# Two outer products and a remainder trade places in the prologue of a fused signature, attention and mixture-of-experts kernel

## The reference

```python
dx = jnp.transpose(x[:, 1:] - x[:, :-1], (1, 0, 2))
def step(levels, v):
    e = [v]
    for k in range(1, d):                       # d = 4
        e.append(_outer(e[-1], v) / (k + 1))
    new = []
    for k in range(d):
        acc = levels[k] + e[k]
        for i in range(k):
            acc = acc + _outer(levels[i], e[k - 1 - i])
        new.append(acc)
    return tuple(new), jnp.concatenate(new, axis=-1)
_, sigs = jax.lax.scan(step, init, dx)
h = jnp.transpose(sigs, (1, 0, 2)) @ W.T + b
```

## Time and profile before

| | before |
|---|---|
| median of 3 runs | 641.4 us (641.23 to 641.78) |
| the profiled execution | 641.93 us |
| its span | 640.1 us |
| PE busy | 615.5 us (96%) |
| DVE busy | 428.1 us (67%) |
| POOL busy | 320.9 us (50%) |
| ACT busy | 289.6 us (45%) |

### The profile page before, as it was taken

How to read it: one execution, slowest core, us unless ns; L and a number is a source line. 1 busy time by engine, 2 the same in 40 slices (tenths; PEclk the granted TensorE clock), 3 DMA queues, 4 the chain that set the end, 5 groups by cost and what they waited for, 6 DMA issues and landing times.

```text
span 640.1 us, 13350 instructions
## 1 busy us (share of the span) xinstructions
PE 615.5 (96%) x4085; PEld 517.7 (81%) x4085; DVE 428.1 (67%) x1093; ACT 289.6 (45%) x640; POOL 320.9 (50%) x336
## 2 busy tenths in 40 slices
PE   6889999999999999999999999999989999999993
PEld 4667888887888887888888787888768999999992
DVE  6977767767777766777776678788556535666450
ACT  4334444544444445343444434444465445666341
POOL 2365544554544454554455455445864502666663
PEclk9999999999999999999999999999999999999998
DMA  8620433344543334343334434111233732434330
GB/s 303 240 106 21 107 82 82 86 117 93 114 116 82 82 97 114 85 108 90 82 82 109 105 90 108 38 37 39 70 93 98 233 105 64 54 58 52 43 47 2
DMA packets 69901, 59.80 MB, mean 93 GB/s; under 512 B 6512, under 2 KB 58608, under 8 KB 69488
## 3 DMA queue, kind: packets, MB, share of 16 engines
q1 hardware_dynamic: 63232, 55.21, 33.3%
q0 software_dynamic: 6640, 4.22, 4.8%
HBM read 16.79 MB, written 26.30 MB: 67 GB/s over the span
## 4 chain that ended last, share of the span: by engine, by line
PE 87%; DVE 6%; POOL 3%; issue 2%; ACT 1%; DMA 0%; SPq 0%; DVEq 0%; POOLq 0%
PE bank L1303 80%; PE bank L1515 2%; PE bank L1360 2%; POOL sorted_rows L510 1%; POOL z L495 1%; POOL z L497 1%; DVE z L923 1%; PE bank L1618 1%; DVE whigh L818 1%; PE bank L1409 1%; PE bank L1418 0%; DVE h L822 0%; PE bank L1364 0%; DMA h<-x_prev 0%; DVE u L868 0%
## 5 line engine op out<-in xcount | busy, mean ns | idle before, releaser
L1303 PE MATMUL bank<-whigh,uth 128*128 128x512 f32 x512 | 167.3, 407 | 1.5 <-issue 1.3
L1303 PEld LDWEIGHTS bank<-whigh,uth 128*128 128x128 f32 x512 | 91.7, 189 | 27.2 <-issue 8.1
L1303 PE MATMUL bank<-whigh,utl 128*128 128x512 f32 x256 | 101.2, 395 | 0.0
L584 POOL DMA_INDIRECT out<-xvo,ids x39 | 61.5, 1577 | 62.9 <-ACT xvo L773 55.8
L504 POOL TENSOR_TENSOR rstd<-rstd,powers 128x1 f32<-128x1 f32 x64 | 35.3, 551 | 113.7 <-DVE rstd L910 65.6
L495 POOL TENSOR_TENSOR z<-z 128x512 f32<-128x512 f32 x32 | 40.8, 1275 | 70.5 <-DVE z L923 70.5
L1303 PE MATMUL bank<-xT,qkw 128*128 128x128 f32 x512 | 63.3, 277 | 0.0
L659 ACT ACTIVATE prob<-prob 128x512 f32<-128x512 f32 x32 | 20.2, 633 | 93.3 <-DVE prob L1050 93.3
L1303 PEld LDWEIGHTS bank<-xT,qkw 128*128 128x128 f32 x512 | 59.6, 192 | 0.7 <-issue 0.4
L1303 PEld LDWEIGHTS bank<-whigh,utl 128*128 128x128 f32 x256 | 48.1, 188 | 11.3
L490 POOL TENSOR_TENSOR e3l<-e,e3h 128x512 fp32r<-128x512 f32 x31 | 40.0, 1292 | 26.8 <-DVE xn L944 26.4
(11 more groups left out here) (236 smaller groups left out, 1364.6 us busy)
## 6 DMA issues: line engine op xcount, KB each, us to landing
sorted_rows<-blank SPq DMA_DIRECT2D x24, 709.5 KB, 6.1
xvp<-xvo SPq DMA_DIRECT2D x128, 128.0 KB, 2.3
w<-w_t SPq DMA_DIRECT2D x1, 4096.0 KB, 12.1
w<-w_high SPq DMA_DIRECT2D x4, 512.0 KB, 6.3
x_columns<-x2t SPq DMA_DIRECT2D x32, 64.0 KB, 1.6
xg_in<-x_columns SPq DMA_DIRECT2D x8, 256.0 KB, 4.1
out<-h SPq DMA_DIRECT2D x8, 256.0 KB, 2.2
levels<-w_t SPq DMA_DIRECT2D x1, 2048.0 KB, 10.5
```

Of the source, the lines that this page charges most:

```text
L584: nc.gpsimd.indirect_dma_start(out=out[:, :], out_offset=bass.IndirectOffsetOnAxis(ap=ids[:, tile:tile + 1], axis=0), in_=y[:, 2 if j == S ...
L1303: return T.matmul(out_, lhsT, rhs, start=start, stop=stop)
```

## The change

Three places move. On DVE, the fourth outer product `level2(3)` goes from behind `level2(2)` to behind `features_lo(0)`. On POOL, in the prologue only and for tile 2 only, the call `level3_rest(2)` is written out with its two operations exchanged, and the remainder no longer waits for `xn_ready`. On DVE, `level4(2)` goes ahead of `add_s2(3)`. No operation is added or removed, and only the order and one wait differ.

```diff
@@ -552,7 +552,11 @@
             add_channels(0)
             level3(2)
             root(0, ln1, 0)
-            level3_rest(2)
+            pool.wait_ge(e3_hi, 3)
+            G.tensor_tensor(e3l[:], e3[:], e3h[:].bitcast(F32), ALU.subtract).then_inc(e3_lo, 1)
+            pool.wait_ge(u4_sb, 2)
+            G.tensor_tensor(by3(g4), spread(g3[:, 2:3, :], 3, [P, 1, C2, CHANNELS]),
+                            spread(vh[:, 2:3, :], 2, [P, 1, C2, CHANNELS]), ALU.mult).then_inc(g4_ready, 1)
             pool.wait_ge(norm_step, SQUARED_STEP)
@@ -892,7 +896,6 @@
             level2(1)
             level4(0)
             level2(2)
-            level2(3)
 
             def one(ap):
@@ -1090,6 +1093,7 @@
             features_lo(0)
+            level2(3)
             signature_lo(0)
@@ -1131,9 +1135,9 @@
             made = nstep(V.tensor_tensor(nrm[:, 3:4], wu_out[:], B[5][:, DIM + 1:DIM + 2], ALU.mult))
             assert made == SUMS_STEP
+            level4(2)
             made = add_s2(3)
             assert made == SMALL_STEPS
-            level4(2)
             x_lo(0)
```

## The result

The changed kernel takes 643.34 us (median of 13 runs, 642.51 to 644.12) against 641.41 us in the same session: ratio 1.0027, 95% interval 1.0018 to 1.0035, so 1.9 us slower (1.2 to 2.2). 643.0 had been forecast, in a range of 641.5 to 643.6. The profiled execution took 643.41 us, its span is 641.6 us.

What follows compares the result with a forecast made beforehand. The prediction took DVE's queue, with POOL between, to bound the prologue. Delays of 0.40 and 1.17 us, with 0 for the third edit, gave 1.57, so 641.4 + 1.6 = 643.0 us, range 641.5 to 643.6 (eight in ten).

Steps and rivals of the forecast that it cites:

- first edit, DVE's queue: Prologue, DVE: with `level2(3)` behind `features_lo(0)`, the next operation starts at 18.01 in place of 17.61, 0.40 us later.
- moved product, duration: DVE at about 17.0 us: outer product `level2(3)`, held by POOL's `e3l` until 17.53, takes about 1.0 us.
- `xn` longer: DVE from 37.17 us: `xn`, held by POOL's `e3l` in place of `g4`, ends at 38.03, 0.21 us later.
- first `nrm`: DVE behind `xn`: the first tiny product, held by POOL's `g4`, takes about 1.1 us rather than 0.15.
- second edit, DVE's queue: DVE at `add_s2(2)`: starts at 39.12 in place of 37.95, 1.17 us later, as is everything up to `weigh(1, 1)`.
- third edit: DVE: `level4(2)` ahead of `add_s2(3)` is the same work in another order and does not wait: 0.
- `accumulate(1)`: PE's piece at 46.80 us, released by POOL behind DVE's `weigh(1, 1)`: comes at 48.4, late by both DVE delays.
- DVE's queue is the bound: Prologue: DVE's queue with POOL between, not PE, bounds it; the rival that PE's waits are the bound, 639.9 us, had 0.06.
- disputed step: DVE behind `xn`: a tiny 128x1 product is held by POOL like a large one; rival, not held, 642.0 us, chance 0.22.
- PE's slack: PE's 0.5 us wait ahead of 46.80: PE's earlier work may shift by some tenths without moving the end.
- the sum: Whole kernel: DVE's delays of 0.40 and 1.17 us add up to 1.57 us, with nothing from `level4(2)`.
- the prediction's last sign of being wrong: PE at 46.80 us: the prediction is wrong if this start moves by anything other than 0.40 + 1.17 = 1.57 us.

Runs made afterwards that it cites:

- g4_waits: The changed kernel with one wait added, so POOL's `g4` of tile 2 may not start before `xn`: 643.07 us against 642.07 for the kernel before, ratio 1.0015.
- fill: The changed kernel with 14 added, unread products in PE's two waits of the prologue: 642.35 us against 641.20 for the kernel before, ratio 1.0014.
- nrm_early: The changed kernel with the three `nrm` products moved ahead on DVE, behind the copy of `wu_out`: 641.51 us against 641.20 for the kernel before, ratio 1.0002.
- b_only: The kernel before with only POOL's `e3l` put ahead of `g4`, without the wait on `xn_ready`: 642.73 us against 642.07, ratio 1.0013.
- e3l: Not a run but a code name: POOL's operation that makes the remainder by subtraction, put ahead of `g4` for tile 2 in the changed kernel.

## Why the prediction held, and where it fell short

| step (us) | forecast | in the trace of the changed kernel |
|---|---|---|
| first edit, DVE's queue | +0.40 | +0.39 |
| moved product, duration | 1.0 | 1.02 |
| `xn` longer | +0.21 | 0.87 for 0.65, +0.22 |
| first `nrm` | 1.1 | 1.04 |
| second edit, DVE's queue | +1.17 | +1.11 |
| third edit | 0 | 0 |
| PE's clock | not thought of | +0.55 |
| `accumulate(1)` | +1.57 | +2.06 |
| median of the runs | +1.6 | +1.9 |

**DVE's queue is the bound.** Shown: PE began its first projection 0.55 us early behind the anchor and waited 1.26 us at `vow` instead. The three edits alone moved DVE's `weigh(1, 1)` by 0.40, 1.05 and 0.70 and `accumulate(1)` by 0.40, 1.62 and 0.70; the 0.57 that are over in the second are the clock's. In all seven changed orders whose trace has the clock up, PE still waited 0.5 us for POOL at `accumulate(1)`.

**The tiny product is held like a large one.** This was the disputed step, with a chance of 0.22 against it. `g4_waits` settles it: the same product at the same place takes 0.15 us when `g4` starts 0.17 later. It is `g4`'s turn that costs, and not the place behind `xn`.

**The step that was wrong** was the sentence that 0.5 us is PE's slack and that "PE's work before it may come earlier or later by some tenths and the end doesn't move". It counted time only. Behind the waits which PE got in exchange for its earlier work, 0.95 and 0.75, the granted clock halved, and PE's work from `xT,qkw` up to `accumulate(1)` took 5.58 us. In `fill`, with the same queues, PE busy and the clock at 1.00, it took 4.51 (43.26 to 48.30, less the wait of 0.53). The 1.07 us between them use up the slack of 0.53 and leave 0.54. So the sum was 0.5 us too small for `accumulate(1)` in this execution, and the prediction's last sign of being wrong, a move of 46.80 by anything other than the sum, came true. The Trainium skill, "TensorE: Matmul & The Clock Gate", part 1, describes a clock of 1.2 or 2.4 GHz set by how busy the engine has recently been; the granted clock of 0.50 here agrees, and I should have set PE's new waits against it.

**How much of the hit is luck.** The interval of the measured ratio, 1.2 to 2.2 us, can't tell the forecast 1.6 from the trace's 2.06. The five runs with the clock up have a median 1.4 us above the kernel before, where the sum of 1.57 belongs, and the eight with the low mean clock 2.0, where 2.06 belongs. The groups overlap, so this is an estimate and not shown: on it, the median came as near as it did because some executions escaped the term that I had left out. The 643.41 us of the profiled execution are near the forecast 643.5 by luck: 0.49 us were missing in the sum, 0.34 came back because the anchor was earlier in this trace, and 0.22 because the part behind `accumulate(1)` was shorter. (The prediction's sentence on the Trainium skill gives the sum as 1.58; its terms add up to 1.57.)

**The third edit** was rightly put at nothing, but for a reason worth keeping: it is free only because of the second. Alone it costs 0.70. The second edit makes the sums on PE early. In `g4_waits` and `nrm_early`, where DVE is hardly held, `level4(2)` doesn't wait for them either (40.16 behind 39.98, and 38.90 behind 38.72).

Two things are open. One is what decides whether the clock falls: by the mean clock it did in 8 of 13 runs of the changed kernel and in 2 of 11 of `b_only`. That it comes from PE's idle time is shown by `fill`; that two waits close together bring it about is not. The other is the scatter behind `accumulate(1)`, of about 1 us between executions of kernels that are the same there, which blurs single ratios.

## What to carry to other kernels

Before moving an operation on VectorE or GpSimd, draw both queues side by side and ask which operation's turn it takes. A wait between two GpSimd operations may be there for what VectorE does in the gap; here the first of three products of one column was held for 0.9 us when it was closed. And where an edit lets TensorE run ahead to a wait, look at the granted clock behind that wait: idle time that is "hidden" can come back as slow time. Look at the clock of every run too, not only of the profiled one, which may be the rarer case.

## What the runs showed of the hardware

- An operation of VectorE with two operands in SBUF, even of 128x1, waits for the rest of a GpSimd operation (1.04 us against 0.15). One that reads a bank doesn't (0.67 beside `g4`). It goes the other way too: POOL's addition took 2.20 us beside DVE's large product and 0.73 without it.
- When both engines have the next operation ready, they alternated here: POOL's `e3l` ended at 38.00, DVE's `xn` at 38.09, POOL's `g4` at 39.03, DVE's `nrm` at 39.05.
- The granted clock fell to 0.50 for 3.4 us behind two waits of TensorE of 0.95 and 0.75 us, 1.4 us apart, and in `b_only` behind 0.95 and 0.90, 0.9 apart. By the mean clock this was so in 8 of 13 runs and in 2 of 11. It stayed at 1.00 behind one of 1.29 us, and behind one of 0.75 us alone.
- With 14 unread products in the two waits it stayed at 1.00 (0.54 us less up to `accumulate(1)`).
